# Two transformer layers on one core: the first two batches' gated products at slots of their own, the FP4 weights by another queue, and the rounding at other slots

## The reference

```python
xn = layernorm(x)
x = x + L0_attn(xn) + L0_ffn(xn)     # softmax attention, 16 heads; FP4 feed-forward
xn = layernorm(x)
x = x + L1_attn(xn) + L1_ffn(xn)     # linear attention; 4 experts, top 2, and a shared one
```

```python
def fp4_quant_dequant(x):
    xb = x.reshape(shape[:-1] + (shape[-1] // 16, 16))
    scale = max(max(abs(xb)) / 6, 1e-12)
    q = GRID[searchsorted(MID, abs(xb / scale))] * sign(xb) * scale
gate, up = linear(fp4(xn), fp4(w_gate)), linear(fp4(xn), fp4(w_up))
y = linear(fp4(silu(gate) * up), fp4(w_down))
```

## Time and profile before

| what | us |
|---|---|
| three runs | 2107.48, 2107.88, 2105.41; median 2107.48 |
| the profiled execution | 2107.8 |
| its span | 2105.3 |
| busy: PE | 1934.3 (92%) |
| busy: DVE | 1540.2 (73%) |
| busy: ACT | 1366.8 (65%) |
| busy: POOL | 1125.6 (53%) |

### The profile page before, as it was taken

One profiled execution on the slowest core, in us unless ns is written; L12 is line 12 of the kernel. 1 busy time (PEld: TensorE's weight loads), 2 busy tenths in 40 slices (PEclk: granted clock), 3 DMA queues, 4 the chain that ended last, 5 costly groups with the idle time before them and its releaser, 6 DMA issues.

```text
span 2105.3 us, 49557 instructions
## 1 busy us (share of the span) xinstructions
PE 1934.3 (92%) x17353; PEld 1264.0 (60%) x17353; DVE 1540.2 (73%) x5223; ACT 1366.8 (65%) x3733; POOL 1125.6 (53%) x1671
## 2 busy tenths in 40 slices
PE   3789999999999999999999999999999999998978
PEld 1455665756566575656657566665656657565645
DVE  7558778687776868778686877868777686876646
ACT  1777585676857667585766858577685766758531
POOL 4675374645637465473746547374563746545220
PEclk9779999999999999999999999999999999999989
DMA  5102021110301112030210202121020111101010
GB/s 146 27 9 44 4 39 23 39 24 9 53 4 38 24 24 38 4 59 3 39 24 18 44 4 44 18 39 24 12 49 4 38 24 20 37 4 34 4 32 6
DMA packets 172651, 59.36 MB, mean 28 GB/s; under 512 B 139643, under 2 KB 169971, under 8 KB 172403
## 3 DMA queue, kind: packets, MB, share of 16 engines
q1 hardware_dynamic: 172403, 56.19, 13.8%
HBM read 14.22 MB, written 4.19 MB: 9 GB/s over the span
## 4 chain that ended last, share of the span: by engine, by line
PE 59%; DVE 14%; ACT 13%; issue 7%; POOL 6%; DMA 0%; SPq 0%; DVEq 0%; ACTq 0%; POOLq 0%
PE ps L1127 11%; PE ps L1198 8%; PE ps L1263 8%; PE ps L1208 7%; PE ps L1141 5%; ACT ring L949 5%; PE ps L1117 4%; DVE ring L583 3%; PE ps L1248 3%; ACT pb L958 3%; PE ps L1186 2%; DVE lin L615 2%; PE ps L1106 2%; PE ps L1174 2%; POOL ring L848 2%
## 5 line engine op out<-in xcount | busy, mean ns | idle before, releaser
L848 POOL TENSOR_SCALAR ring<-ring,row_rcp,tau_row 128x128 f32<-128x128 f32 (+3 forms) x1024 | 626.5, 620 | 681.4 <-DVE row_rcp L590 681.4
L949 ACT ACTIVATE ring<-ring,neg_max 128x128 f32<-128x128 f32 (+3 forms) x1024 | 570.7, 558 | 514.7 <-DVE neg_max L583 504.6
L1127 PE MATMUL ps<-identf,ring 128*128 128x128 f32 x2560 | 380.1, 287 | 5.9 <-POOL ring L848 4.0
L958 ACT ACTIVATE pb<-ps 128x512 f32<-128x512 f32 x640 | 348.4, 583 | 25.2 <-PE ps L1127 21.1
L583 DVE CUSTOM_DVE_ANT_1 ring<-ps,bias_t 128x384 f32<-128x384 f32 (+1 forms) x496 | 286.7, 614 | 54.3 <-PE ps L1117 47.0
L1127 PEld LDWEIGHTS ps<-identf,ring 128*128 128x128 f32 x2560 | 279.0, 143 | 78.6 <-issue 42.7
L1263 PEld LDWEIGHTS ps<-ed_t,h 128*128 128x128 f32 (+1 forms) x1920 | 254.6, 191 | 97.2 <-issue 93.7
L1263 PE MATMUL ps<-ed_t,h 128*128 128x128 f32 (+1 forms) x1920 | 270.6, 277 | 0.0
L1208 PE MATMUL ps<-xn1T,eu_t 128*128 128x512 f32 (+1 forms) x480 | 256.5, 616 | 1.4 <-DVE h L639 1.3
L1198 PE MATMUL ps<-xn1T,eg_t 128*128 128x512 f32 (+1 forms) x480 | 254.8, 612 | 3.1 <-DVE h L632 2.8
L1117 PE MATMUL ps<-qkT 32*128 32x128 f16 (+3 forms) x1024 | 201.5, 308 | 47.2 <-DVE neg_max L583 28.2
(11 more groups left out here) (150 smaller groups left out, 2771.8 us busy)
## 6 DMA issues: line engine op xcount, KB each, us to landing
x_t<-x SPq DMA_DIRECT2D x16, 256.0 KB, 2.8
x<-x SPq DMA_DIRECT2D x16, 256.0 KB, 2.9
o_rows<-o_stack SPq DMA_DIRECT2D x256, 16.0 KB
out<-x SPq DMA_DIRECT2D x16, 256.0 KB, 2.3
qkT<-qkx SPq DMA_TRANSPOSE x128, 3.2
...
```

Source lines behind the costliest of these rows:

```text
L848: pool.tensor_scalar(e, e, row_rcp[:, m % 2, r:r + 1], tau_row[:, i, HG * g + r:HG * g + r + 1], ALU.mult, ALU.add).then_inc(p_ok.sem, 1)
L949: act.activation(e, e, ACT.Exp, bias=neg_max[:, n % 2, r:r + 1], scale=-1.0, accum_out=row_sum[:, n % 2, r:r + 1]).then_inc(exp_ok.sem, 1)
L958: act.activation(pb[:, c % NPB, :], bank(turn_bank(q)), ACT.Relu).then_inc(t_taken[q % 2].sem, 1)
L1127: last = pe.transpose(o[:, r * P:(r + 1) * P], ring_of(i, r)[:, k * P:(k + 1) * P], idf)
```

## The change

Instead of one table of places for all batches there are three: one for batch 0, one for batch 1 and one for all later ones, and `hidden_at(b)` picks it wherever a place of the hidden values' work is asked for. The weights are loaded by ScalarE's DMA queue, and DVE quantizes them in slots 0, 2 and 4 of frame -1. The copy of the identity in float16 (`ident16`, L507), which nothing read, is gone, and with it one increment of `s_set`. PE and ACT turn and store the weights still at slot 11 of frame -1, though the place is now written `QKV0 + T`.

```diff
-GATE0 = (11, 13, 16, 18)
-HID_AMAX, HID_STEP, HID_SCALED = (18, 19, 34, 35), 36, (38, 39, 40, 41)
-HID_MAGIC, HID_ADD, HID_SUB, HID_MUL = (48, 50, 52, 54), (56, 58, 60, 62), (57, 59, 61, 63), (64, 66, 68, 70)
-TURN_H, FUTURE_V, FUTURE_Y = (ATT + 11, ATT + 13, ATT + 13, ATT + 15), ATT + 61, ATT + 63
+HIDDEN = (
+    dict(gate=(64, 66, 68, 70), amax=(73, 74, 75, 76), step=77, scaled=(78, 79, 80, 81), magic=(82, 84, 86, 88),
+         add=(84, 86, 88, 90), sub=(85, 87, 89, 91), mul=(90, 92, 94, 96), turn=(ATT + 35, ATT + 35, ATT + 37, ATT + 39)),
+    dict(gate=(42, 44, 47, 49), amax=(50, 51, 52, 53), step=54, scaled=(55, 56, 57, 58), magic=(57, 58, 59, 60),
+         add=(59, 60, 61, 62), sub=(60, 61, 62, 63), mul=(64, 66, 68, 70), turn=(ATT + 11, ATT + 13, ATT + 13, ATT + 15)),
+    dict(gate=(11, 13, 16, 18), amax=(18, 19, 34, 35), step=36, scaled=(38, 39, 40, 41), magic=(42, 43, 44, 45),
+         add=(44, 46, 48, 50), sub=(45, 47, 49, 51), mul=(52, 54, 56, 58), turn=(ATT + 11, ATT + 13, ATT + 13, ATT + 15)),
+)
+FUTURE_V, FUTURE_Y = ATT + 61, ATT + 63
...
+def hidden_at(b):
+
+    return HIDDEN[min(b, len(HIDDEN) - 1)]
...
-            for dst, src in fp4_weights:
-                sp.dma_start(dst, src).then_inc(s_wload.sem, 16)
...
                 if s == 0:
                     dve.wait_ge(s_first.sem, N_FIRST)
-                    dve.tensor_copy(ident16[:, :], identf[:, :]).then_inc(s_set.sem, 1)
-                if s == 4:
                     dve.wait_ge(s_wload.sem, N_WLOAD)
                     dve.wait_ge(s_set.sem, 3)
                     fp4_steps(W, q_step, BW, s_wq, 0)
                     dve.wait_ge(s_wq.sem, 3)
                     dve.tensor_tensor(blocks(W), blocks(W), by_block(q_step[:, 0, 0:BW]), ALU.mult).then_inc(s_wq.sem, 1)
-                if s == 6:
+                if s == 2:
...
-                if s == 7:
+                if s == 4:
...
         def _(act):
+            for dst, src in fp4_weights:
+                act.dma_start(dst, src).then_inc(s_wload.sem, 16)
...
-                if f == -1 and s == GATE0[0]:
+                if f == -1 and s == QKV0 + T:
                     turn_weights()
+                if f == 0 and s == 0:
                     pe.wait_ge(s_wTs.sem, 4)
-                if f == 0 and s == 0:
                     pe.wait_ge(s_late.sem, N_LATE)
-                    pe.wait_ge(s_set.sem, 5)
+                    pe.wait_ge(s_set.sem, 4)
```

More of the change, by code:

```diff
@@ L128, in __init__ @@
                         gate_ticket(("qkv", layer, b, p - p0), (p - p0) % 2)
-                for layer, places in enumerate((GATE0, GATE1)):
+                for layer, places in enumerate((hidden_at(b)["gate"], GATE1)):
                     if p in places:
@@ L1280, in beside @@
                         up(layer, b, places.index(p - 1))
-                for name, t in at((("hid", TURN_H),), p):
+                for name, t in at((("hid", hidden_at(b)["turn"]),), p):
                     turn_hidden(b, t)
```

42 lines of the change are left out of this document (20 added, 22 removed).

## The result

The change made the kernel slower. Its median is 2121.52 us (2119.89 to 2122.24, four executions), beside 2107.68 us for the kernel before on the same chip: 1.0065 times as long, 95% interval 1.0052 to 1.0078. The forecast was 2098.7, in a range from 2089.5 to 2108.0. Three executions of two kernels further down (one of c_magic_early_pool_old, two of h_weights_alone) took more than 2600 us, and the medians and ratios there leave them out. The profiled execution took 2121.33 us with a span of 2119.3, against 2105.3 before, so the spans differ by 14.0 us, and these I now divide.

What follows compares the result with a forecast made beforehand. PE was taken to bound fourteen of the sixteen attention frames. Start -15.9, frame 0 +6.8 and repeated frame 0 sum to -9.1 us against 2107.8, giving 2098.7, range 2089.5 to 2108.0.

Steps and rivals of the forecast that it cites:

- the repeated frame: Frames counted fourteen times: rounding moved earlier, priced at nothing, with 0.3 us per frame either way.
- the repeated frame loses: Rival: magic numbers beside POOL in slots 42 to 45 overfill DVE, 1.35 us a frame, 2117.7 us; chance 0.09.
- The first score: End of the start: DVE takes it near 36.2 instead of 52.05 us, giving back 15.9, between 14 and 18.
- the second end of the bounds: Start: weight pieces run quicker without POOL beside them, so the first low half begins some 4 to 5 us earlier.
- Frame 0: First frame, now with two batches' hidden values and without the leftovers: +6.8 us, bounds 0 and +14.
- (c): Frame 0, steps 5 to 7: batch 0's POOL operations and the scalings need 16.6 us against 13.6, so +3.0.
- (d): Frame 0, step 15: batch 1's squeeze, four first multiplications of 0.80 us on a full POOL, +3.2.
- The leftovers: Frame 0: batch 1's reciprocal root no longer waits on POOL behind batch 0's rounding, 1.9 us gone.
- (a): Frame 0 gates: two of batch 0's cost +1.5 us; batch 1's move from steps 2 to 4 to 10 to 12, net nothing.
- (b): Frame 0, slots 9 to 13: batch 0's largest values and steps on DVE, some 2.9 us, part behind scores, +1.
- pays part of it: Head of frame 1: batch 1's last multiplications and batch 2's norm wait for POOL, paying part of the +3.2 us squeeze.
- The lock: DVE and GpSimd's shared port pair as an exclusive lock; the rows were said not to agree in a whole instruction's wait.

Runs made afterwards that it cites:

- c_magic_early_pool_old: The change, but for batches 2 and later only the magic numbers move; POOL's add, sub and last multiplication stay at the old slots 56 to 70: 2104.06 us.
- h_weights_alone: The kernel before with only the weights' part: loads by ScalarE's queue, quantization in slots 0, 2 and 4, no float16 identity: 2106.15 us.
- d: The change with POOL's add, sub and last multiplication four slots later for batches 2 and later, magic numbers still at 42 to 45: 2101.54 us.
- a: The change with batches 2 and later back at the old rounding slots, magic numbers and POOL's part alike: 2103.53 us.
- k: The change with POOL's add, sub and last multiplication two slots later for batches 2 and later: 2107.12 us in one run.
- e: From d: batch 0's gates, largest values and steps back ahead of frame 0, batch 1's gates to rounding moved, its additions at the old places: 2103.90 us.
- f: From d: the three pieces of the weights' quantization in slots 2, 4 and 9 instead of 0, 2 and 4: 2102.65 us.

## Why the prediction was wrong

**The step that failed** is the one whose sign the prediction named as decisive, frames that move by more than 0.3 us: "I take nothing, with 0.3 us per frame either way", in the part on the repeated frame. The frames moved by 1.37 us each, because DVE's magic numbers waited for POOL's instructions beside them. What came is the rival that had 0.09: the repeated frame loses. It was priced at half of 2.7 us, 1.35 a frame; measured, 1.37. Two reasons stood against it. The first, that POOL was busy for only 5.1 of 17.8 us in steps 10 and 11, was read from a stretch of the kernel before, into which the change puts POOL's own new work: it is busy for 9.02 of 19.50 us now. DVE's magic numbers and POOL's additions that consume them follow one another by two slots in the table, so once POOL had work there the meeting was not rare. The second, that as much is taken out of slots 48 to 54, was right for the magic numbers alone, as c and d show: what step 10 loses by them (0.8 us), steps 11, 12 and 0 give back. It said nothing of POOL's additions, and what those cost in step 11, nothing gave back. The rival itself was right in the sum and wrong in how, so that 1.35 meets 1.37 is luck: not eight magic numbers at 0.82 with half of the excess on the path, but four of eight held up, 1.39 us over the 3.02 of c and d, and nearly all of it on the path.

**The first score** was forecast at 36.2, measured at 35.4: 16.7 us gained for 15.9. The low half came at 25.7 (25 to 29 named). The chain was as priced, the shift 2.8 late for 2.5; DVE's pieces took the second end of the bounds more than the first, since only the last multiplication ran beside POOL (2.06 us).

**Frame 0** was forecast at +6.8 and came to +7.2, by groups of four steps -0.8, +3.6, +3.9 and +0.6. (c), POOL's work in steps 5 to 7, was forecast at +3.0; steps 4 to 7 gave +3.6, with POOL busy for 23.17 of 23.20 us. That the sums agree is in part luck, since a term of 3.2 us, (d), did not fall in this frame at all. The leftovers gave about what was forecast: the reciprocal root of batch 1 begins 1.9 us after the first score for 3.5, and step 0 is 1.0 us shorter. (a), that batch 1's gates leave steps 2 to 4 and come back in 10 to 12 at no net cost, is what the steps show: -2.6 us in steps 2 to 4 and +2.6 in steps 10 and 11; batch 0's two gates in step 1 cost 2.6 (5.7 to 8.3) in this profile and 0.8 (6.5) in a's, which is the same program in that step, beside the 1.5 forecast. Between this profile and those of a, c, d and k, with the same program in this frame, the two groups in the middle agree within 0.4 us, but the first took 26.5 to 27.9 us there for 28.7 here and the last 21.4 to 22.3 for 19.8, with the granted clock (0.77 in this frame) low in other places. So only the middle two are firm, and (b) cannot be told apart in them. (d), the squeeze of batch 1, was forecast at +3.2 in step 15; step 15 got shorter by 0.8, steps 14 and 15 together took 10.8 us for 10.6, and the bill came at the head of frame 1, whose step 0 takes 11.6 us for 8.7. POOL's timeline shows it behind by 4.2 us at the start of frame 1 (129.1), where it had been 1.4 before (the end of the row at 139.04 is 139.98, 1.4 after 138.6):

```profile
132.41 0.92 POOL L891 TENSOR_TENSOR hid<-hid,q_m 128x352 f32<-128x352 f32 x1
```

PE's waits for POOL in that step, now and then before:

```profile
PE ps L1134 <- POOL ring L853: 3.8, 2, 2.1
```

```profile
PE ps L1127 <- POOL ring L848: 1.7, 1, 1.7
```

So 2.1 of the +2.9 is PE waiting longer for POOL; in the rest PE is busy for 7.75 us instead of 6.80, at a granted clock of 0.50 instead of 0.70. The +2.9 the prediction had only as something that "pays part of it", so for the head of frame 1 it is an underestimate of 3 us; e, with the squeeze undone, has that step at 8.7 again. The rest of frame 1's +4.3 is its share of the repeated loss: its steps 10 to 12 take 27.8 us for 26.4. (In a these steps are at 26.4 again and frame 1 is at 131.7 all the same: its step 1 took 8.2 us there for 6.9, at a granted clock of 0.54 for 0.64.)

**Frame 15** had of the moved rounding only the last multiplications, in steps 0 and 1, which take 5.51 and 5.99 us in both kernels. Of its +1.4, 1.1 is the clock's: in its step 5 PE ran at a granted clock of 0.50 (1.2 GHz) for 4.7 us, and before at 0.57 for 4.0, while in kernel a that step had 1.00 and took 6.5 us for 9.3 and 8.1.

```profile
1929.30:1934.00 4.70, 4.70 (x35) 3.63 (x36) 0.84 (x5) 2.53 (x7) 1.31 (x3) 0.50 0.01 3
```

**The sum again**: -16.7 + 7.2 + 2.9 + 14 x 1.37 + 1.4 = +14.0. Without the repeated frame's 19 it would be -5, beside -9.1 forecast; kernel a, which is that kernel, is 3.4 us faster by its medians and 5.6 by its span.

**The lock.** The prediction quoted the Trainium skill, SBUF — State Buffer, section "SBUF: two separate sides", for an exclusive lock between DVE and GpSimd, and said that the rows do not agree in a whole instruction's wait. That reading was wrong: by the page, where a DVE operation needs the shared port pair, whichever engine starts first has the pair until its own instruction is over, and the other is blocked that long. The rows above agree with that: a magic number begun while POOL's instruction runs ends 0.20 us after POOL's end, and f's two pairs take turns. So does the very row that the prediction quoted, the addition of 2.26 us at 19.06. POOL's row beside it, of the kernel before:

```profile
18.50 1.64 POOL L867 TENSOR_TENSOR xq<-xq,q_m 128x512 f32<-128x512 f32 x1
```

POOL's instruction ended at 20.14 and the addition at 21.32, 1.18 us behind, the same distance as L528's in f. What it waits for is the rest of the instruction that holds the port, so the price for a magic number lies between nothing and one POOL instruction, here up to 0.6 us. Taken seriously, that rule would have asked at each magic number which POOL instruction runs at that moment, and the answer was in the new order of the instructions.
